# A third buffer for the gate/up weights of a recurrent block with a gated feed-forward, and one buffer shared by two stages to make room for it

## The reference, cut to what matters

```python
xn = layernorm(x)                                   # x: (2, 16384, 1024)
# recurrent part; h starts at 0 for each batch
u = xn @ W_in.T + b_in
h[t] = exp(lambda_log) * h[t-1] + gamma * u[t]
s = h @ W_out.T + b_out + xn
# gated feed-forward, int weights times 1/127
f = (silu(xn @ wg.T) * (xn @ wu.T)) @ wd.T          # hidden size 3072
out = x + s * silu(f)
```

## Time and profile before

| | |
|---|---|
| median of 2 runs | 1360.57 us (1356.16 to 1364.97) |
| the profiled execution | 1361.04 us |
| its span, slowest core (core 3) | 1359.5 us |
| spans of cores 0 to 7 | 1352.2, 1347.5, 1350.6, 1359.5, 1347.6, 1342.7, 1340.8, 1352.4 us |
| mean granted TensorE clock, lowest and highest core | 0.993, 0.998 |
| TensorE matmuls busy | 1294.2 us, 95% |
| VectorE, ScalarE, GpSimd busy | 26%, 21%, 15% |
| DMA | 190.90 MB, mean 140 GB/s |

### The profile page before, as it was taken

One profiled execution on the slowest core, in us unless ns is written; L12 is line 12 of the kernel. 1 busy time (PEld: TensorE's weight loads), 2 busy tenths in 40 slices (PEclk: granted clock), 3 DMA queues, 4 the chain that ended last, 5 costly groups with the idle time before them and its releaser, 6 DMA issues.

```text
span 1359.5 us, 15876 instructions; the slowest of 8 cores (1340.8 to 1359.5 us)
## 1 busy us (share of the span) xinstructions
PE 1294.2 (95%) x6032; PEld 589.6 (43%) x6032; DVE 349.2 (26%) x566; ACT 290.5 (21%) x437; POOL 198.6 (15%) x198
## 2 busy tenths in 40 slices
PE   0899999999998999999999999999999999999997
PEld 0544445444453445444454344544445444454443
DVE  2222311324012240223302232022320334013322
ACT  2511023110231112311222112211123110231100
POOL 1000031300321003300033001230021200331002
PEclk9999999999999999999999999999999999999999
DMA  9954305742066410864127540474305642065301
GB/s 219 264 163 143 111 32 187 233 139 92 32 216 217 155 62 32 258 209 152 32 88 251 187 155 7 149 245 157 124 16 202 222 151 93 31 232 171 124 1 62
DMA packets 124798, 190.90 MB, mean 140 GB/s; under 512 B 3507, under 2 KB 101939, under 8 KB 124724
## 3 DMA queue, kind: packets, MB, share of 16 engines
q1 hardware_dynamic: 101524, 103.90, 24.2%
q0 software_dynamic: 23200, 85.99, 19.3%
HBM read 177.29 MB, written 16.78 MB: 143 GB/s over the span
## 4 chain that ended last, share of the span: by engine, by line
PE 89%; DMA 7%; DVE 1%; issue 1%; ACT 1%; SPq 0%; DVEq 0%; ACTq 0%; POOL 0%; POOLq 0%
PE pb L337 24%; PE pb L291 22%; PE pb L299 22%; PE pb L319 9%; PE pb L268 9%; DMA wgubuf<-wgu_t 6%; PE pb L249 2%; PE pb L314 1%; DMA ones_sb<-ones 1%; DVE stats L189 0%; ACT xnb L230 0%; DVE hbT L462 0%; SPq L156 0%; ACT guT L383 0%; DVE xbuf L490 0%
## 5 line engine op out<-in xcount | busy, mean ns | idle before, releaser
L291 PE MATMUL pb<-xnbT,wgubuf 128*128 128x512 bf16 x1536 | 366.5, 382 | 21.1 <-DMA wgubuf<-wgu_t 15.5
L299 PE MATMUL pb<-xnbT,wgubuf 128*128 128x512 bf16 x1536 | 363.8, 380 | 0.0
L337 PE MATMUL pb<-wdfull,hbT 128*128 128x512 bf16 x1536 | 332.8, 379 | 0.0
L462 DVE SCALAR_TENSOR_TENSOR hbT<-pb,siluT 128x512 bf16<-128x512 f32 x192 | 132.8, 692 | 591.3 <-PE pb L299 591.3
L291 PEld LDWEIGHTS pb<-xnbT,wgubuf 128*128 128x128 bf16 x1536 | 149.2, 98 | 209.9 <-issue 37.0
L394 ACT ACTIVATE siluT<-pb 128x512 bf16<-128x512 f32 x192 | 114.8, 598 | 562.7 <-PE pb L291 559.5
L299 PEld LDWEIGHTS pb<-xnbT,wgubuf 128*128 128x128 bf16 x1536 | 150.7, 98 | 182.6 <-issue 2.6
L337 PEld LDWEIGHTS pb<-wdfull,hbT 128*128 128x128 bf16 x1536 | 150.3, 98 | 181.3
L531 POOL TENSOR_TENSOR gslab<-gslab,s_sb 128x512 bf16<-128x512 bf16 x60 | 72.3, 1205 | 830.2 <-ACT gslab L352 823.8
L268 PE MATMUL pb<-xnbT,winT 128*128 128x512 bf16 (+1 forms) x576 | 122.8, 375 | 3.6 <-ACT guT L383 3.6
L319 PE MATMUL pb<-woutT,guT 128*128 128x512 bf16 x512 | 121.6, 380 | 0.0
(11 more groups left out here) (29 smaller groups left out, 243.3 us busy)
## 6 DMA issues: line engine op xcount, KB each, us to landing
wgubuf<-wgu_t SPq DMA_DIRECT2D x96, 1024.0 KB, 5.9
wdfull<-wd_t POOLq DMA_DIRECT2D x32, 1536.0 KB, 15.9
out<-xbuf POOLq DMA_DIRECT2D x32, 512.0 KB, 3.0
xbuf<-xe POOLq DMA_DIRECT2D x7, 2048.0 KB, 12.3
winT<-win_t POOLq DMA_DIRECT2D x2, 1024.0 KB, 14.3
xbuf<-xe SPq DMA_DIRECT2D x1, 2048.0 KB, 18.1
woutT<-wout_t POOLq DMA_DIRECT2D x1, 2048.0 KB, 17.3
xbuf<-xe SPq DMA_DIRECT2D x2, 512.0 KB, 8.0
```

The source lines that it names most:

```text
L291: O("tensor", lambda eng, g=g, cc=cc, kc=kc, gb=gb: eng.matmul(pb[gb][:, 0:512], wgubuf[g % 2][:, kc * 512 + cc * 128: kc * 512 + cc * 128 ...
L299: O("tensor", lambda eng, g=g, cc=cc, kc=kc, ub=ub: eng.matmul(pb[ub][:, 0:512], wgubuf[g % 2][:, kc * 512 + 256 + cc * 128: kc * 512 + 25 ...
L337: O("tensor", lambda eng, c=c, m=m, n=n: eng.matmul(pb[2 * m + n][:, 0:512], hbT[:, c * T + m * 128: c * T + m * 128 + 128], wdfull[:, c * ...
L462: O("vector", lambda eng, c=c: eng.scalar_tensor_tensor(hbT[:, c * T:(c + 1) * T], pb[3 + 2 * (c % 3)][:, 0:512], QINV, siluT[c % 2][:, :] ...
```

## The change

The buffer `wgubuf` gets a third part with a semaphore of its own, and SyncE's load of group G waits for TensorE's group G-3 in place of G-2. The two `siluT` buffers (128 x 512, bf16) are no longer of their own: they are the first two of the four `gslab` buffers. Since output blocks 4 and 5 of the tile before use these, ScalarE's silu of blocks 0 and 1 of each tile from the second on waits for GpSimd's combine of those output blocks. The small f32 buffer `bout_sb` (one partition) now lies in the last quarter of `xnb`; it is read once, at the start. Nothing is added to or taken from the arithmetic.

```diff
-    wgubuf = [sb(f"wgubuf{i}", [128, NK * 512], BF16) for i in range(2)]
+    wgubuf = [sb(f"wgubuf{i}", [128, NK * 512], BF16) for i in range(3)]
...
-    siluT = [sb(f"siluT{i}", [128, T], BF16) for i in range(2)]
     gslab = [sb(f"gslab{i}", [128, T], BF16) for i in range(4)]
+    siluT = gslab[:2]
...
-    bout_sb = sb("bout_sb", [1, D], F32)
...
+    bout_sb = xnb[0:1, 3 * D:4 * D]
...
-              "s_xh0", "s_xh1", "s_xh2", "s_seta"):
+              "s_xh0", "s_xh1", "s_xh2", "s_seta", "s_wgu2"):
...
-                            wgubuf[g % 2][:, kc * 512 + cc * 128: kc * 512 + cc * 128 + 128],
+                            wgubuf[g % 3][:, kc * 512 + cc * 128: kc * 512 + cc * 128 + 128],
...
-                            wgubuf[g % 2][:, kc * 512 + 256 + cc * 128: kc * 512 + 256 + cc * 128 + 128],
+                            wgubuf[g % 3][:, kc * 512 + 256 + cc * 128: kc * 512 + 256 + cc * 128 + 128],
...
                 if c >= 2:
                     W("scalar", mark=("gumul", k, c - 2))
+                elif k >= 2:
+                    W("scalar", mark=("comb", k - 1, 4 + c))
...
-                if G >= 2:
-                    k2, g2 = (G - 2) // NGU + 1, (G - 2) % NGU
+                if G >= 3:
+                    k2, g2 = (G - 3) // NGU + 1, (G - 3) % NGU
                     W("sync", mark=("umm", k2, 2 * g2 + 1))
...
-                dst = wgubuf[G % 2][:, :].rearrange("p (kc h) -> p kc h", h=512)
-                O("sync", lambda eng, s=src, d=dst: eng.dma_start(d, s),
-                  inc=f"s_wgu{G % 2}", n=16, mark=("wgu", G))
+                dst = wgubuf[G % 3][:, :].rearrange("p (kc h) -> p kc h", h=512)
+                O("sync", lambda eng, s=src, d=dst: eng.dma_start(
+                    d, s), inc=("s_wgu0", "s_wgu1", "s_wgu2")[G % 3], n=16,
+                    mark=("wgu", G))
```

## The result

| | before | changed |
|---|---|---|
| median | 1357.5 us (10 runs) | 1336.7 us (11 runs) |
| ratio, with its 95% interval | | 0.983 (0.980 to 0.986) |
| span of the slowest core, profiled execution | 1359.5 us (core 3) | 1334.2 us (core 4) |
| fastest core | 1340.8 us | 1328.5 us |

The forecast was 1333 us, with a range of 1329 to 1342. The change makes the kernel 1.7% faster; more runs of the kernel before moved its median from 1360.6 to 1357.5 us.

A forecast was written before the change was run, and what follows sets the result against it. TensorE, busy 95% of 1359.5 us, was taken as the bound. From 1361.0 us: minus 28.2 for late loads, minus 1.1 for small hold-ups, plus 1.4 for the new wait, gives 1333.1, so 1333 us; range 1329 to 1342.

The forecast's parts named there:

- Late loads are the whole loss in the tiles: TensorE at L291, gate/up: late `wgubuf` loads cost 28.2 us, 20.7 of it idle; the third buffer removes all.
- small hold-ups: Gate to output projection, even in the quiet last tile: 0.15 to 0.2 us a tile, taken as 1.1 for eight tiles.
- The third buffer has slack enough: Gate/up loads get 13.8 us in place of 6.9; the longest found behind the start is 11.0, so none is late.
- meet no new traffic: Gate/up loads are issued at the same moments as before, each for a group one further ahead.
- The new wait: Silus of gate blocks 0 and 1 wait for GpSimd's output blocks 4 and 5, delaying block 3: 1.4 us, bounds 0 and 12.
- bites in every tile: Rival: cores stay in step, `wdfull` lands late everywhere, seven stalls of 1.7 us at block 3: 1344 us; chance 0.12.
- The start, `bout_sb`, the third load at the start: Before the first gate matmul and in `xnb`: third 1 MB load and `bout_sb` sharing cost 0; without cover, 5.9 us once.
- How fast `wdfull` loads: By the skill's 358 GB/s, 6.3 MB take 17.6 us, so no new wait, 1331.7 us, chance 0.18; trace shows 24.1.
- Bandwidth as the limit: Rival at the gate/up loads: memory is short, the third buffer passes the wait on; half stays, 1347 us; chance 0.07.
- slower: Rival: block 3 stall passes 2.3 us, the clock falls, 4.0 us a tile eats the gain; 2% slower is 1388; chance 0.02.

The follow-up runs named there:

- second run: The changed kernel again, unaltered, on the same chip as the kernel with silu written into `hbT`: 1335.7 us, 0.984 of before.
- the silu in `hbT`: Changed kernel, but gate's silu is written into its place in `hbT` and multiplied there, without `siluT` and its GpSimd wait: 1332.5 us; beside the changed kernel 1333.6.
- the sharing alone: Kernel before with two gate/up buffers, `siluT` put into `gslab` with its wait on GpSimd's combine: 1360.7 us beside 1361.8, ratio 0.998.

## Why the prediction was right, point by point

**Late loads are the whole loss in the tiles: right.** The prediction took 20.7 us of idle time and 7.5 us of clock and restarts away on core 3, and 1.1 us of small hold-ups, 29.3 in all. From the first gate matmul (68.76) to the end core 3 took 1290.7 us before; a core without waits takes 1261.4 now, which is 29.3 less. Gate to down is 100.1 us where no new wait stands, 0.15 below the quietest tile before. That the waits booked on `hbT` in the earlier trace rows were loads is shown too: they went with the loads, and with the silu in `hbT` nothing stands there at all.

**The third buffer has slack enough: right, by less than thought.** The prediction looked at the loads of the kernel before, at most 11.0 us. In the changed kernel core 6 has one of 11.6 and in its second run core 2 one of 12.0, and the kernel with the silu in `hbT` has 13.5 of 13.8. That the loads "meet no new traffic" was the weak step. It is true of one core's own order of transfers. Between the cores it changes: counted from each core's own start, the last x load was issued within 19 us of each other on the eight cores before, within 10 in the changed kernel and within 4 with the silu in `hbT`. That this meeting makes the loads longer fits the numbers, but no run held everything else and changed it alone.

**The new wait: mechanism and working right, size too small.** It was put at 0.2 us a tile, 1.4 in all. Core 0, which never waits there, takes 1261.4 us from its first gate matmul (67.14) to the end; core 4 takes 1267.3, of which 5.0 are idle. So the term was 5.9 us on the core that decides. The sum for the profiled execution then closes: 1333.1 + 4.5 for this term - 1.9 because core 4 starts gate earlier than the core of the sum = 1335.7, which is what it took. The weak step is the choice of the value from core 3. For core 3 itself it was right: that core takes 1262.5 us, 1.1 more than a core without the wait. It was right for the average core too, since the idle times at block 3 of the eight cores (0, 2.1, 0, 0.2, 5.0, 1.0, 0 and 3.1 us) have a mean of 1.4. But the metric is the slowest core, and so the largest of eight such sums counts.

Why the waits are larger than core 3's old trace said is shown in part. GpSimd's timeline on core 3 in the last tile, before and after:

```profile
1193.19 0.85 POOL L517 DMA_DIRECT2D wdfull<-wd_t  x1 [12.53 <-PE pb L249]
```

```profile
1165.91 3.33 POOL L520 DMA_DIRECT2D wdfull<-wd_t  x4 [12.55 <-PE pb L249]
...
1190.27 1.15 POOL L538 TENSOR_TENSOR xbuf<-xbuf,gslab 128x512 f32<-128x512 f32 x1 [19.45 <-issue]
```

Before, the add came 21.9 us behind the first `wdfull` issue (1215.11); after, 24.4 us. An add up to about 24.1 us behind it costs nothing. Over the eight cores the mean was 24.4 us in tile 2 of the kernel before and 22.9 in its later tiles, when its stalls had pulled the cores apart; it is 24.7 and 23.8 in the changed kernel. That fits cores that stay in step. But the old trace also had late adds when the first issues of the eight cores lay up to 19 us apart: in the last tile 25.1 us on core 0 and 25.8 on core 4, and on core 0 none of the seven came before 24.0. So part of the term could have been read from the other cores, and being in step as the cause of the rest is argued, not shown. On core 4 in tile 2 of the changed kernel the add came 26.2 us behind the first issue, where the latest seen before was 25.8, one of the things by which the prediction said it would be wrong. The wait there was 1.9 us where 1.7 was the most expected, and the tile lasted 160.9 us where 159.3 was. The rival "bites in every tile" was too high in price: core 4 pays in five tiles, cores 0, 2 and 6 never.

**Which core is slowest: wrong.** The sum was made for core 3, the slowest before. It again starts gate last, 2.9 us later than core 4, but it waited only 0.2 us and ended 1.9 us earlier. That the forecast came within 4 us of the median has some luck in it: the 4.5 us missing in the wait were partly met by the 1.9 us of the earlier start.

**The start, `bout_sb`, the third load at the start: right.** The start's waits are those of before (first input on core 4: 23.4 us, before 23.8; on core 3: 25.5 us, before 25.7), and the first gate matmul stands at 66.5 to 69.8 us on the eight cores, before at 66.2 to 68.8.

**How fast `wdfull` loads.** In tile 2 on core 4 the 6.3 MB took from the first issue at 209.0 to 211.5 + 23.4 = 234.9, 25.9 us, 243 GB/s (issues and us to landing of its `wdfull` loads):

```profile
L520 POOL DMA_DIRECT2D wdfull<-wd_t x4: 829/836/851, 209.0 to 211.5; - x4
...
DMA to landing us min/median/max: 10.6/16.6/23.4
```

The first 3 us of these moved 7 GB/s, the 4 us from 220 to 224 moved 350 GB/s, and the last 3 us 139. The Trainium skill (HBM Reference, section Specifications (TRN2)) gives about 358 GB/s a core with both cores of a pair streaming, and at that rate from first issue to last landing no wait would be left. The trace agrees with it as the rate of the fastest stretches, the 350 GB/s here and the 343 GB/s over 7 us of the run with `wdfull` loaded once, but not as the mean over the loads, which is what the wait goes by.

**Bandwidth as the limit: excluded** for the changed kernel. The run that moved the x load shows that most of the loss, 20.5 us there, could be won without any buffer, by moving one transfer.

## What to carry to other kernels

Price a new wait for the core where it comes latest, over all cores and tiles of the trace, and not for the core that is slowest now: its mean over the eight cores was the forecast's 1.4 us, and the core that decided paid 5.9. When a deeper buffer takes stalls away from cores that run one program, they also drift apart less, and the longest load may grow (here from 11.0 to 13.5 us), so leave it more slack than the old trace asks for. Before adding a buffer, look what is in flight beside the long loads: here one wait in front of a 2 MB load won as much (0.984 of before) as the change with its 1 MB of buffer (0.983). And writing in place did away with the wait of the shared buffer: that kernel (1332.5 us, 0.978 of before) needs 5 to 6 us less on the core that paid most, of which the time of an execution showed 2.1 us on one chip. It and the other variants with three buffers and no wait at block 3 (0.977 to 0.981) can't be told apart by time.

## What the runs showed of the hardware that was not expected

Behind a drain GpSimd goes on only when the transfers that it issued itself have landed: 21.3 us idle with `wdfull` open on its queue, 0.23 us with the same loads issued by SyncE. In that run the drain behind a store of 0.5 MB took 7.0 us.

Taking about a quarter of the bytes away made the kernel before slower, 1371.5 against 1361.8 us. The x load came to stand beside a gate load, and moving the x load alone made the kernel faster, 1341.4 against 1361.9.

How long TensorE stands does not by itself tell whether its clock falls. In the kernel before on core 3 it fell behind a wait of 2.30 us (274.87) and not behind one of 2.23 (603.02). With the sharing alone it fell behind one of 1.98 us (core 4, 433.31); with `wdfull` loaded once and two buffers it stayed at 1.00 behind one of 3.43 (core 0, 892.25). So the 2.3 us by which the prediction priced its rival "slower" are one case and not a bound.
